# First half of the second feed-forward product's first sum in one lump early in the block, its other half later

## The chip, the cores and the metric

The kernel runs on one core of one Trainium2 chip. The metric is the device time of one execution in microseconds (us). The kernel before was run three times: 4296.52, 4300.87 and 4306.44 us, median 4300.87 us. One more execution, of 4298.3 us, was profiled, and all rows shown here come from it.

## The reference

A block of a transformer on x of shape (8, 1024, 512): eight sequences, called samples here, of 1024 tokens.

```
y   = x + attention(layernorm(x))        # differential attention, 16 heads, causal
out = y + (gelu(layernorm(y) @ W1q.T + b1) @ W2q.T + b2)
```

The attention projects queries (32 sub-heads of 16), keys and values, applies rotary embedding, takes two causal softmaxes a head, subtracts the second times a scalar from the first, multiplies by the values, normalises each head's output and projects with Wo. The feed-forward part has 2048 hidden features; W1q and W2q are the weights rounded to -1, 0 or 1, and gelu is the exact one.

## The kernel before, in words

A **block** is one tile of 128 query tokens against all keys up to it: 8 tiles a sample, t0 to t7, 64 blocks. The width of a row of scores grows from 128 in t0 to 1024 in t7. All five engines run the same list of blocks and meet by semaphores alone; within an engine the order is fixed by the program (a plain loop over **half heads**, numbered 0 to 31 in each block, two a head), so an instruction that waits holds up all that is behind it on its engine.

In each half head TensorE makes scores ahead (`SP_`, lines 852 and 853), VectorE takes the row's maximum (`NM`, 682 or, for t0 to t3 in pairs, 690), ScalarE the exponential (`E`, 554), VectorE subtracts the two softmaxes (`E`, 705), TensorE transposes the difference (`DP` and, from t4 on, `DX`, 864), ScalarE copies it (`DT`, 566), and at the end of each eight heads TensorE multiplies it by the values (`M`, 887). Score slots are few (four banks), so scores of a later softmax wait for the exponential of an earlier one.

Between these stand, at fixed half heads, the pieces of other work for neighbouring tiles: layernorm, transposes and projections of the next tile's queries, keys and values (`M` from `TOK`, `T`, and line 837 from `WQKV`), the previous tile's output (transposes of `T`, product with `WO`), and the feed-forward part, which is done for two tiles together (a **pair**):

- In odd blocks, the first product (line 909, into `F`): 8 pieces of two feature tiles (f) each, at the half heads `W1_AT`. The piece at half head `at` computes its first f there, its second at `at + 1`, and ScalarE empties both at `at + 2` (`HP`, line 613). One f is 8 matmuls. Each piece after the first waits until the one before has been emptied.
- Gelu on ScalarE (line 571), eight feature tiles at once: for the first half in half head 14 of the odd block (`GELU_ODD`), for the second half in half head 0 of the even block after it (`GELU_EVEN`). Each time it is between two loads of activation tables. GpSimd then splits each quarter of a half into a high and a low part (`HH`, `HP`, `HL`, lines 470, 472, 474), at half heads 15 to 18 of the odd block and 1 to 4 of the even one.
- In even blocks, the second product (line 924, into `F`): two **sums** j = 0 and 1 (one per tile of the pair), each over 16 f, with two matmuls an f (`HH` and `HL` against `W2Q`). The sums start at the half heads `W2_AT = (4, 18)` and are spread over 13 half heads, so one f or two in each. f 8 to 15 of the first sum wait for GpSimd's split of the second half (`h_ready`). VectorE takes the finished sum out of `F` (line 774) at half heads 17 and 31.

`F` is a single bank. Its users are in turn: the eight pieces of the first product, sum 0, sum 1. In TensorE's program a piece of either product stands behind the half head's transposes and projections and ahead of `scores_ahead` or `half_v`. At even half heads the order is: scores, transposes of differences, the second part of the value product, the layernorm and projection work, the feed-forward piece, the scores of the next head. The second product runs in 32 even blocks: t4 and t6 of the first sample, t0, t2, t4 and t6 of seven more, and two in the tail behind the last attention block.

Of the kernel before, what the change touches and what calls it, by code (L numbers as in the profile page):

```python
# [49 lines left out]
FT = FF // P  # L50
# [15 lines left out]
GELU_F = FT // 2  # L66
# [53 lines left out]
MEAN_SQ, RMS_ROWS, AN_TURN = 10, 14, 23  # L120
O_PROJ, O_SUM = (24, 25, 26, 27), 28
LN2_STATS, LN2_ROWS, LN2_TURN, LN2_REST = 28, 30, 31, 31
W1_AT = (1, 4, 7, 11, 15, 19, 23, 27)
GELU_ODD, GELU_EVEN = 14, 0
SPLIT_ODD, SPLIT_EVEN = (15, 16, 17, 18), (1, 2, 3, 4)
W2_AT, W2_N = (4, 18), 13
OUT_AT = (17, 31)


class QBlock:  # L130
# [25 lines left out]
    def first_product(self, hs):  # L156

        for k, at in enumerate(W1_AT if self.w1 else ()):
            if hs in (at, at + 1, at + 2):
# [2 lines left out]

    def second_product(self, hs):

        for j, at in enumerate(W2_AT if self.w2 else ()):
            if at <= hs < at + W2_N:
                return j, range(FT * (hs - at) // W2_N, FT * (hs - at + 1) // W2_N)
        return None


# [11 lines left out]
def diff_attention_ffn(nc, x, wqT, wkT, wvT, woT, lams, subw, w1T, b1, w2T, b2, rope, out):  # L182
    ctx = ExitStack()
    with ctx:
# [156 lines left out]
        def hold(eng, signal, value):  # L341


            if not isinstance(value, int) or value > 0:
                eng.wait_ge(signal, value)
                eng.sem_inc(held, 1)
# [480 lines left out]
        def _(pe):  # L827
# [85 lines left out]

            def second_product(q, j, fs):

                if fs[0] == 0:
                    hold(pe, h_ready, 8 * q + 4)
                    hold(pe, hp_ready, 8 * q + 8)
                    hold(pe, o_sum, 2 * q + j)
                for f in fs:  # L920
                    if f == GELU_F and j == 0:
                        hold(pe, h_ready, 8 * q + 8)
                    for hp in (HH, HL):
                        ins = pe.matmul(F[:, :], hp[:, f, P * j:P * (j + 1)], W2Q[:, f, :],  # L924
                                        start=(f == 0 and hp is HH), stop=(f == FT - 1 and hp is HL))
                if fs[-1] == FT - 1:
                    ins.then_inc(f2_ready, 1)

            def pe_work(T):
                b, t, nb, nf = T.b, T.t, T.nb, T.nf  # L930
                for hs in range(HS_TILE):
# [57 lines left out]
                    if T.second_product(hs):  # L989
                        second_product(T.pair, *T.second_product(hs))  # L990
# [67 lines left out]
```

## Time and profile before

| | before |
|---|---|
| runs | 4296.52, 4300.87, 4306.44 us |
| profiled execution, its span | 4298.3 us, 4296.5 us |
| mean granted TensorE clock | 0.926 |
| busy: TensorE, VectorE, ScalarE, GpSimd | 81%, 79%, 67%, 33% |
| wait of scores for an exponential (TensorE) | 385.4 us in 218 waits |

Busy shares are means over stages of a block that have different limits; a stage is read from the timeline of its own stretch. The timeline gives start and duration of an instruction in us, the engine, the line, the operation, what it writes and reads, the shapes, and in square brackets how long the engine was idle before it and what ended that. The windows view gives for a stretch its length, and for each engine the busy time and the number of instructions, then the granted clock (1.00 is 2.4 GHz, 0.50 is 1.2 GHz), the share of the DMA engines and GB/s.

### The profile page before, as it was taken

To read this page: it belongs to the slowest core of one execution; us is meant where nothing else is said; L and a number is where in the kernel's file an instruction comes from. 1 tells how busy PE (TensorE), PEld (TensorE's weight loads), DVE (VectorE), ACT (ScalarE), POOL (GpSimd) and SP (SyncE) were. 2 spreads that over 40 slices of the span, in tenths; PEclk is the share of its full clock that TensorE was granted. 3 is DMA by queue.
4 is the path that set the end of the run, shared out by engine and by line. 5 is a ranking of instruction groups with operands and counts; after the bars stand their busy time and mean duration, and the time that the engine had idled before them with its cause. 6 is when DMAs were issued, how large, how long until landed. Compare 5 with 4: busy or idle time off the path is not lost.

```text
span 4296.5 us, 81536 instructions
## 1 busy us (share of the span) xinstructions
PE 3484.7 (81%) x23454; PEld 2095.0 (49%) x23454; DVE 3382.8 (79%) x6194; ACT 2880.2 (67%) x6784; POOL 1437.2 (33%) x1564
## 2 busy tenths in 40 slices
PE   2688888888888887888788888888878878888886
PEld 1355544455445454545544544445544555444553
DVE  6788977888678886888767887778877889778881
ACT  1577766777567775677756777667766777567772
POOL 1243233332332324433343323432234432333323
PEclk6899999999999999999999999999999999999998
DMA  3100011000011001100011000101011000111000
GB/s 130 41 18 30 19 33 33 31 17 29 25 33 33 18 30 33 33 20 28 21 33 33 26 27 18 39 25 33 20 34 33 25 23 20 34 33 33 15 29 12
DMA packets 146817, 128.38 MB, mean 30 GB/s; under 512 B 66608, under 2 KB 117680, under 8 KB 145840
## 3 DMA queue, kind: packets, MB, share of 16 engines
q1 hardware_dynamic: 146352, 122.79, 8.8%
q8 instruction: 218, 3.57, 0.3%
q14 instruction: 247, 2.02, 0.2%
HBM read 67.61 MB, written 55.12 MB: 29 GB/s over the span
## 4 chain that ended last, share of the span: by engine, by line
PE 41%; DVE 20%; issue 20%; ACT 12%; POOL 5%; DMA 1%; SPq 1%; DVEq 1%; ACTq 1%; POOLq 0%
PE M L837 9%; DVE NM L682 6%; PE M L887 6%; PE SP_ L852 6%; PE F L924 6%; PE F L909 5%; PE DP L864 4%; DVE NM L690 3%; ACT E L554 3%; ACT DT L566 2%; ACT L571 2%; PE M L831 2%; DVE CC L702 1%; PE DX L864 1%; PE SP_ L853 1%
## 5 line engine op out<-in xcount | busy, mean ns | idle before, releaser
L554 ACT ACTIVATE E<-SP_,NM 128x256 f32<-128x256 f32 (+7 forms) x2048 | 1520.4, 743 | 1020.3 <-DVE NM L690 533.8
L852 PE MATMUL SP_<-KST,QST 96*128 96x512 f16 (+3 forms) x3072 | 838.2, 344 | 459.2 <-ACT E L554 385.4
L682 DVE TENSOR_REDUCE NM<-SP_ 128x1 f32<-128x896 f32 (+3 forms) x1024 | 1031.9, 1017 | 225.0 <-PE SP_ L853 218.5
L705 DVE SCALAR_TENSOR_TENSOR E<-E,CC 128x512 f32<-128x512 f32 (+7 forms) x1024 | 942.2, 920 | 36.2
L864 PE MATMUL DP<-ident,E 128*128 128x128 f32 x3328 | 585.1, 292 | 112.8 <-DVE E L705 97.2
L852 PEld LDWEIGHTS SP_<-KST,QST 96*128 96x128 f16 x3072 | 277.9, 101 | 793.8 <-ACT E L554 531.1
L690 DVE TENSOR_REDUCE NM<-SP_ 128x2 f32<-128x1024 f32 (+3 forms) x512 | 419.4, 819 | 244.8 <-PE SP_ L853 239.5
L566 ACT ACTIVATE DT<-DP 128x512 f32<-128x512 f32 (+3 forms) x1024 | 524.8, 513 | 127.8 <-PE DP L864 121.4
L837 PE MATMUL M<-WQKV,WT 128*128 128x512 f32 x1040 | 538.4, 611 | 10.3 <-DVE TOK L746 5.3
L909 PE MATMUL F<-X2H,W1Q 128*128 128x256 f16 x2048 | 501.4, 283 | 39.4 <-ACT HP L613 21.7
L864 PEld LDWEIGHTS DP<-ident,E 128*128 128x128 f32 x3328 | 389.8, 149 | 277.8 <-issue 125.8
L909 PE MATMUL F<-X2L,W1Q 128*128 128x256 f16 x2048 | 499.7, 282 | 0.0
L853 PE MATMUL SP_<-maskb,identb 128*128 128x128 bf16 x2048 | 450.9, 229 | 0.0
L450 POOL TENSOR_TENSOR RST<-VE,nhalf 128x1 f32<-128x1 f32 x129 | 70.9, 549 | 1113.8 <-DVE VE L644 1113.8
L554 ACT ACTIVATION_READ_ACCUMULATOR E<-SP_,NM 128x1 f32 x2048 | 413.0, 202 | 0.0
L924 PE MATMUL F<-W2Q,HH 128*128 128x512 fp8e4 x1024 | 389.8, 381 | 15.6 <-POOL HL L474 10.1
L924 PE MATMUL F<-W2Q,HL 128*128 128x512 fp8e4 x1024 | 388.9, 380 | 0.0
L887 PE MATMUL M<-DT,V 128*32 128x256 f32 x4608 | 318.5, 414 | 22.4 <-ACT DT L566 21.6
L474 POOL TENSOR_TENSOR HL<-HP,HH 128x512 f16<-128x512 f32 x256 | 318.3, 1243 | 21.4
L702 DVE TENSOR_SCALAR CC<-R,SUM,neglam 128x1 f32<-128x1 f32 x1024 | 279.3, 273 | 39.2 <-DVE R L700 2.1
L853 PEld LDWEIGHTS SP_<-maskb,identb 128*128 128x128 bf16 x2048 | 210.1, 103 | 182.2 <-issue 42.7
L837 PE MATMUL M<-WO,WT 128*128 128x512 f32 x512 | 271.8, 613 | 4.1 <-ACT WT L600 3.0
(94 smaller groups left out, 4726.9 us busy)
## 6 DMA issues: line engine op xcount, KB each, us to landing
scratch<-SPL SPq DMA_DIRECT2D x65, 576.0 KB, 2.8
QST<-scratch SPq DMA_DIRECT2D x390, 64.0 KB, 2.4
X<-in_x SPq DMA_DIRECT2D x66, 256.0 KB, 2.7
out<-SQ SPq DMA_DIRECT2D x64, 256.0 KB, 2.0
KST<-scratch SPq DMA_DIRECT2D x390, 32.0 KB, 1.9
DT<-in_w2T SPq DMA_DIRECT2D x1, 4096.0 KB, 25.7
KST<-in_w1T SPq DMA_DIRECT2D x2, 1024.0 KB, 12.0
WQKV<-in_wqT SPq DMA_DIRECT2D x1, 1024.0 KB, 7.1
```

The costliest lines, as they stand in the source:

```text
L554: act.activation(dst, score_out(i, 2 * n + k, w), ACT.Exp, bias=NM[:, (2 * u + k) % 8:(2 * u + k) % 8 + 1], scale=1.0, accum_out=SUM[:, i ...
L566: act.activation(DT[:, k0:k1, n % HALF, :], (DP, DX)[g][:, 0:P * (k1 - k0)].rearrange("p (k q) -> p k q", q=P), ACT.Copy).then_inc(dt_read ...
L682: nc.vector.tensor_reduce(NM[:, m:m + 1], score_out(i, 2 * n + k, P * (i + 1)), AX.X, ALU.max, negate=True).then_inc(max_ready, 1)
L690: nc.vector.tensor_reduce(NM[:, m:m + 2], SP_[:, k:k + 2, 0:P * (i + 1)], AX.X, ALU.max, negate=True).then_inc(max_ready, 2)
L705: nc.vector.scalar_tensor_tensor(out=E1[:, u % 4, 0:w], in0=E2[:, u % 2, 0:w], scalar=CC[:, u % 4:u % 4 + 1], in1=E1[:, u % 4, 0:w], op0=A ...
L837: ins = pe.matmul(M[:, :], WT[:, P * j:P * (j + 1)], w[:, j, c0:c0 + 512], start=(j == 0), stop=(j == KD - 1))
L852: pe.matmul(SP_[:, k[a // 512], 0:n], q, KST[0:ROWS, a // P:(a + n) // P, kk, :], start=True, stop=not last)
L853: ins = pe.matmul(SP_[:, k[(w - P) // 512], (w - P) % 512:(w - P) % 512 + P], identb[:, :], maskb[:, :], start=False, stop=True)
L864: ins = pe.transpose((DP, DX)[g][:, P * (k % 4):P * (k % 4 + 1)], E1[:, u % 4, P * k:P * (k + 1)], ident[:, :])
L887: ins = pe.matmul(M[DV * q:DV * (q + 1), 0:2 * P], V[:, k, v:v + DV], DT[:, k, 2 * q:2 * q + 2, :], start=(k == 0), stop=(k == i), skip_gr ...
L909: ins = pe.matmul(F[:, 2 * P * j:2 * P * (j + 1)], W1Q[:, c, P * f:P * (f + 1)], xp[:, c, :], start=(c == 0 and xp is X2H), stop=(c == KD ...
L924: ins = pe.matmul(F[:, :], hp[:, f, P * j:P * (j + 1)], W2Q[:, f, :], start=(f == 0 and hp is HH), stop=(f == FT - 1 and hp is HL))
```

## The change

Of the first sum (j = 0) of the second product, f 0 to 7 (16 matmuls) are issued together in half head 1 of the even block, and f 8 to 15 in half heads 10 to 16: one f each in 10 to 15 and two in 16. The second sum stays at 18 to 30. In odd blocks the pieces 4, 5 and 6 of the first product start at half heads 16, 20 and 24 in place of 15, 19 and 23.

```diff
-W1_AT = (1, 4, 7, 11, 15, 19, 23, 27)
+W1_AT = (1, 4, 7, 11, 16, 20, 24, 27)
-W2_AT, W2_N = (4, 18), 13
+W2_LUMP, W2_REST, W2_NEXT = 1, (10, 7), (18, 13)
...
     def second_product(self, hs):
-        for j, at in enumerate(W2_AT if self.w2 else ()):
-            if at <= hs < at + W2_N:
-                return j, range(FT * (hs - at) // W2_N, FT * (hs - at + 1) // W2_N)
+        if not self.w2:
+            return None
+        if hs == W2_LUMP:
+            return 0, range(0, GELU_F)
+        for j, f0, (at, n) in ((0, GELU_F, W2_REST), (1, 0, W2_NEXT)):
+            if at <= hs < at + n:
+                return j, range(f0 + (FT - f0) * (hs - at) // n, f0 + (FT - f0) * (hs - at + 1) // n)
         return None
...
             def second_product(q, j, fs):
+                if not fs:
+                    return
                 if fs[0] == 0:
```

## Rows read from the trace of the kernel before

**Rows 1.** The page: busy us of each engine.
```profile
PE 3484.7 (81%) x23454; PEld 2095.0 (49%) x23454; DVE 3382.8 (79%) x6194; ACT 2880.2 (67%) x6784; POOL 1437.2 (33%) x1564
```

**Rows 2.** Waits of TensorE: us in total, times, longest.
```profile
PE SP_ L852 <- ACT E L554: 385.4, 218, 5.5
PE F L924 <- POOL HL L474: 10.1, 2, 9.3
```

**Rows 3.** Windows, blocks t0, t2, t4, t6: TensorE done with half head 0, until released.
```profile
1607.90:1615.70 7.80, 1.13 (x6) 0.73 (x5) 3.86 (x11) 6.43 (x10) 2.38 (x4) 0.50 0.00 1
1712.50:1718.50 6.00, 1.16 (x5) 0.58 (x4) 2.59 (x6) 5.94 (x9) 2.03 (x4) 0.50 0.00 0
1829.00:1834.10 5.10, 0.02 (x1) 0.00 (x1) 1.83 (x5) 5.06 (x6) 2.31 (x4) 0.50 0.00 0
1968.20:1973.70 5.50, 0.02 (x1) 0.00 (x0) 2.61 (x5) 5.46 (x6) 2.51 (x4) 0.50 0.00 0
```

**Rows 4.** Windows, the same blocks: from that release until the clock rises.
```profile
1615.70:1619.90 4.20, 4.20 (x36) 2.57 (x40) 3.46 (x7) 2.17 (x8) 3.57 (x5) 0.50 0.02 4
1718.50:1722.30 3.80, 3.32 (x22) 1.61 (x23) 3.62 (x8) 2.08 (x8) 3.44 (x4) 0.50 0.00 0
1834.10:1838.40 4.30, 4.06 (x30) 2.43 (x34) 3.37 (x6) 2.09 (x5) 3.86 (x5) 0.51 0.03 6
1973.70:1978.30 4.60, 4.58 (x28) 2.70 (x32) 3.44 (x5) 3.08 (x7) 4.16 (x5) 0.50 0.02 4
```

**Rows 5.** Windows, the same blocks, half heads 5 to 12.
```profile
1623.00:1635.00 12.00, 11.51 (x63) 6.16 (x62) 7.65 (x22) 4.96 (x23) 6.58 (x6) 1.00 0.01 3
1723.10:1735.80 12.70, 11.91 (x63) 6.58 (x62) 10.13 (x21) 7.41 (x23) 8.43 (x9) 1.00 0.00 1
1841.20:1856.00 14.80, 13.76 (x78) 7.65 (x77) 13.72 (x26) 10.03 (x26) 7.14 (x6) 1.00 0.00 1
1982.00:1998.00 16.00, 15.80 (x90) 9.02 (x89) 15.50 (x25) 12.56 (x26) 5.97 (x4) 1.00 0.01 2
```

**Rows 6.** Timeline, second product at the full and at the half clock.
```profile
1628.01 0.38 PE L924 MATMUL F<-W2Q,HH 128*128 128x512 fp8e4 x1
1628.23 0.38 PE L924 MATMUL F<-W2Q,HL 128*128 128x512 fp8e4 x1
...
4279.34 0.63 PE L924 MATMUL F<-W2Q,HH 128*128 128x512 fp8e4 x1
4279.76 0.63 PE L924 MATMUL F<-W2Q,HL 128*128 128x512 fp8e4 x1
```

**Rows 7.** Timeline, block t0: behind the release, then to the query projection.
```profile
1615.69 1.11 PE L864 MATMUL DX<-ident,E 128*128 128x128 f32 x4 [3.67 <-ACT DT L566]
1617.16 3.26 PE L887 MATMUL M<-DT,V 128*32 128x256 f32 x32
1620.61 1.93 PE L887 MATMUL M<-DT,V 128*32 128x256 f32 x32
...
1623.69 0.60 PE L831 MATMUL M<-ident,TOK 128*128 128x128 f32 x4
...
1626.65 1.10 PE L837 MATMUL M<-WQKV,WT 128*128 128x512 f32 x2 [0.39 <-DVE TOK L746]
```

**Rows 8.** Timeline, block t2: GpSimd's last split; second product in half head 10.
```profile
1727.07 1.16 POOL L474 TENSOR_TENSOR HL<-HP,HH 128x512 f16<-128x512 f32 x1
...
1732.33 0.38 PE L924 MATMUL F<-W2Q,HH 128*128 128x512 fp8e4 x1
```

**Rows 9.** Timeline, VectorE: one instruction away from and beside GpSimd's split.
```profile
1139.34 0.54 DVE L648 TENSOR_SCALAR TOK<-X,MV,RST 128x512 f32<-128x512 f32 x1
...
1837.00 1.38 DVE L648 TENSOR_SCALAR TOK<-X,MV,RST 128x512 f32<-128x512 f32 x1
```

**Rows 10.** Timeline, block t5: TensorE's waits in half heads 16 and 18.
```profile
1930.97 0.82 PE L852 MATMUL SP_<-KST,QST 96*128 96x512 f16 x2 [2.81 <-ACT E L554]
...
1937.70 0.50 PE L852 MATMUL SP_<-KST,QST 96*128 96x512 f16 x2 [1.34 <-ACT E L554]
```

## The prediction

> **What bounds the kernel now.** I read the page first, then TensorE's waits, then windows and timelines of one sample's even blocks (t0, t2, t4, t6 of the fourth; the blocks repeat in all seven samples of the loop). TensorE is busy 3484.7 of 4296.5 us and VectorE 3382.8 [rows 1], so neither is the bound by its sum alone; where each is has to be read by stage. The longest wait of TensorE is that of scores for an exponential, 385.4 us in all, with a longest of 5.5 [rows 2]. The windows show where it lies: in each even block TensorE is through with half head 0 and then has next to nothing to do for 5.1 to 7.8 us, while ScalarE is busy all along (5.06 of 5.10 in t4) with a table load, the gelu of half a hidden tile, and another table load [rows 3]. In this stretch the granted clock is 0.50, and after the release it stays there for another 3.8 to 4.6 us although TensorE is then almost always busy (4.20 of 4.20 us in t0) [rows 4]. Behind that, in half heads 5 to 12, TensorE is the busiest engine: 11.51 of 12.00 us in t0, 11.91 of 12.70, 13.76 of 14.80, and 15.80 of 16.00 in t6 [rows 5]. But VectorE closes up on it: idle for 4.35 us of that stretch in t0, 2.57 in t2, 1.08 in t4, 0.50 in t6. So work taken from TensorE there pays in full in t0 at best, and in t6 hardly.
>
> **The lump.** It adds nothing and removes nothing: 16 matmuls a block go from half heads 4 to 9 (seven f) and 12 (one f; half head 10 keeps one) to half head 1. Two matmuls of this kind start 0.22 us apart at the full clock and 0.42 at the half [rows 6], so the lump takes 16 x 0.215 = 3.4 us or 16 x 0.425 = 6.8 us. What it needs is there: f 0 to 7 were split in the odd block before, and `F` was emptied at half head 29 of it. The clock is at 0.50 when the lump starts. In the four rows it rose 4.20, 3.80, 4.30 and 4.60 us after TensorE had resumed [rows 4]; I take 4.2 us, that is 10 matmuls at 0.425, and 6 at 0.215: 5.5 us. Bounds are 3.4 and 6.8.
>
> The room for it, less what TensorE did in it: 7.80 - 1.13 = 6.7 us in t0, 6.00 - 1.16 = 4.8 in t2, 5.1 in t4, 5.5 in t6 [rows 3]. So with 5.5 us the lump overruns by 0.7 in t2, 0.4 in t4 and not in t0 and t6; behind it wait the scores and transposes of half head 2, and for these ScalarE's copy and VectorE's maximum. This is more than given back by the clock, which is now at 1.00 when that work comes. In t0, the value product of 32 matmuls took 3.26 us at the half clock and 1.93 at the full one a moment later, and the four transposes ahead of it 1.11 against 0.60 for four of the same shape at the full clock (line 831) [rows 7]; 1.33 + 0.51 = 1.8 us earlier. All of it would be on TensorE's path in t0, since the next scores stand behind the value product. In t2 it is half of that product (16 matmuls, 0.7 us saved), in t4 and t6 VectorE has its own queue there. I take head gains of 1.8 us in t0, 0.3 net in t2, 0.6 in t4 and 0.5 in t6 (bounds: 0 and 1.8 each, and minus 2.0 if the clock does not come up, below).
>
> The same VectorE instruction took 0.54 us away from GpSimd's split and 1.38 us beside it in t4's head [rows 9]. The Trainium skill, "SBUF — State Buffer", section "Who interferes with whom", says that VectorE and GpSimd share one pair of ports and that whichever starts first keeps the other out for the whole instruction. By that rule of the Trainium skill alone VectorE would be held to GpSimd's pace in the heads of t4 and t6, the splits being where they were, and the head gains of these two would be 0 in place of 0.6 and 0.5; the sum below would be 4298.3 - 43 = 4255 us for the profiled execution.
>
> **The relief in half heads 4 to 12.** One f costs TensorE 2 x 0.215 = 0.43 us there; eight are 3.4 us a block. Not all of it is on the path. From the layernorm transposes of half head 6 (1623.69) to the query projection (1626.65) are 2.96 us in t0 [rows 7]: transposes 0.60, copy on ScalarE 0.60, transposes of the attention output, VectorE's multiplication, each waiting for the one before; two f stand in it and fill waits. Without them TensorE waits 0.86 us more, so these two give nothing. For the f of half head 12 I count nothing either, since the key projection behind it needs VectorE's rotation of the queries (bounds 0 and 0.43). That leaves five f, 2.15 us. In t0 VectorE has 4.35 us of slack and takes it; I deduct 0.6 for ScalarE, whose copy at half head 6 stands behind an exponential: 1.8 + 2.15 - 0.6 = 3.3 us. In t2 the slack is 2.57 us, of which part is round trips that stay; I take 1.0 and with the head 1.3. In t4 VectorE's slack is 1.08: 0.6 here, 1.2 with the head. In t6 0.50: 0.3, and 0.8 with the head. Each is bounded by 0 and by 2.15 + 0.43 + 0.86 = 3.4.
>
> **The other half.** f 8 now stands in half head 10, one earlier, and waits for GpSimd's last split. In t2, where this is closest, that split ends at 1728.2 and the second product of half head 10 is at 1732.3 [rows 8], so with f 8 there and 1.5 us earlier it has 2.6 us to spare. It costs nothing, unless half head 10 comes over 4 us earlier. In the tail, f 8 waits for GpSimd as it is (two waits, 10.1 us [rows 2]) and all of the lump's gain ends in that wait: 0.
>
> **Pieces 4 to 6 of the first product.** In each odd block one f (8 matmuls) leaves the gelu stretch of half head 15 and goes to half head 17, another goes from 19 to 21. TensorE's wait in half head 16 grows by 0.87 us (2.81 us in t5), at no cost, since the release is the exponential. The f now in half head 17 delays the scores of 18 by 0.87 us, but the wait of 1.34 us in the same half head absorbs that [rows 10], and ScalarE empties `F` one half head later, so that the exponential for which TensorE waits comes up to 0.8 us sooner. Against it: a longer gap, after which the clock may fall where it did not. I take +0.5 us a sample for the four odd blocks together, bounds -3 and +3.
>
> **Sum.** 3.3 + 1.3 + 1.2 + 0.8 + 0.5 = 7.1 us a sample, times 7 = 49.7; the first sample has t4, t6 and their neighbours only: 2.3. Together 52 us. 4298.3 - 52 = 4246 for the profiled execution, 2.6 us below the median of the runs, so 4249 us against a median of 4300.9.
>
> **The rivals.**
> 1. TensorE is the bound all through, and VectorE's slack is no limit. Then 3.4 us of relief in each of 30 blocks, 102 us, less the two f of the latency chain (26 us), and the heads (3.2 us a sample, 24 us): 100 us, 4201 us. For it: TensorE's busy share in rows 5. Against it: VectorE's, in t4 and t6.
> 2. VectorE and the round trips are the bound outside t0, and heads are eaten by the overrun. Then t0 alone gives 2 to 3.3 us: 7 x 2.5 = 18 us, 4283 us. For it: VectorE's 13.72 of 14.80 and 15.50 of 16.00 us. Against it: the slack that it still has in t2.
> 3. Slower: the clock stays at the half through the lump. It takes 6.8 us in a room of 6.7, 4.8, 5.1 and 5.5: overruns of 0.1, 2.0, 1.7 and 1.3 us, which hold scores and transposes of half head 2 and with them every engine. 7 x 2.1 + 8 x 3.0 = 39 us, and the relief is lost because VectorE starts late and cannot catch up: 4340 us. It decides from the point where the overrun (5.1 us a sample) exceeds the relief that VectorE can take. Against it: a lump is denser than what raised the clock in rows 4.
> 4. No change that can be told: the gains of t0 go into later waits of the same block, and odd blocks lose as much. 4299 us.
>
> **How the numbers follow.** Forecast 0.63, rival 1 0.14, rival 2 0.11, rival 3 0.07, rival 4 0.05. What a measurement of this kernel can tell from no change is 0.2%, 8.6 us. Faster: 0.63 + 0.14 + 0.10 = 0.87; within 0.2%: 0.06; slower: 0.07. The forecast's own range is 4225 to 4275 by the bounds on t2, t4 and t6; with the better part of rivals 1 and 2, 4207 to 4285.
>
> **What would show it.** In the changed profile: 16 matmuls of line 924 in a row inside the gelu stretch of each even block, the last six or so 0.22 us apart; the granted clock at 1.00 from half head 2 on, and the 32-matmul value product of t0 at 1.9 us; a longer wait for the attention-side multiplication ahead of t0's query projection, over 1 us in place of 0.39; VectorE nearly gapless in t6; the mean granted clock above 0.926. Block t0 shorter by 3.3 us, t6 by 0.8, odd blocks as before. The prediction is wrong if the first scores of half head 2 come later by more than 1 us in t2 or t4, if f 8 waits for `HL` inside the loop, or if the odd blocks get longer by over 0.5 us each.

## The result, and the profile after

The changed kernel takes 4275.64 us (median of 4 runs, 4273.97 to 4279.57), against 4303.65 for the kernel before beside it (4 runs, 4296.52 to 4306.97): a ratio of 0.9938, interval 0.9925 to 0.995. That is 28 us faster, 4276 where 4249 was forecast. The side was right, the size only about half of the forecast's 52 us, and the time lies at the edge of the forecast's own range, 0.6 us above its upper end of 4275 (it is inside the wider 4207 to 4285, which takes in the better part of rivals 1 and 2). The profiled execution took 4276.51 us, with a span of 4274.7 us and a mean granted clock of 0.946.

The page after, busy us of each engine, to be read against [rows 1]:

```profile
PE 3496.3 (82%) x23454; PEld 2087.9 (49%) x23454; DVE 3397.1 (79%) x6194; ACT 2883.5 (67%) x6784; POOL 1440.0 (34%) x1564
```

The counts of instructions are the same, and each engine's busy time is within 15 us of what it was. Nothing was taken off an engine; work was moved into waits. TensorE's waits after, to be read against [rows 2] (line numbers are 4 higher in the changed kernel):

```profile
PE SP_ L856 <- ACT E L558: 341.4, 271, 3.8
...
PE M L891 <- ACT DT L570: 47.5, 59, 2.0
...
PE F L930 <- POOL HL L478: 14.6, 2, 9.3
PE M L841 <- ACT WT L604: 12.1, 16, 1.0
...
PE F L930 <- issue: 8.8, 6, 2.8
```

The scores' wait fell by 44 us, to a longest of 3.8. Three waits grew: those of the value product for its copy (21.6 us before), of the products of line 841 for theirs (3.0 before) and of `F` for `HL` (10.1 before, again two, both in the tail). The windows of the gelu stretch, same blocks as [rows 3]:

```profile
1602.50:1611.30 8.80, 5.84 (x23) 2.41 (x21) 3.87 (x11) 6.44 (x10) 2.39 (x4) 0.64 0.00 1
1704.50:1710.70 6.20, 5.68 (x23) 2.31 (x21) 2.71 (x8) 6.14 (x9) 2.12 (x4) 0.74 0.00 0
1820.60:1825.80 5.20, 5.17 (x19) 1.78 (x16) 1.93 (x5) 5.16 (x6) 2.31 (x4) 0.69 0.00 0
1956.80:1962.40 5.60, 5.28 (x19) 1.89 (x18) 2.68 (x5) 5.56 (x6) 2.55 (x4) 0.70 0.01 3
```

Here as in all windows the first pair of times is the stretch, then come its length and the busy time of TensorE, of its weight loads, of VectorE, ScalarE and GpSimd, and the granted clock. TensorE is now busy for 5.17 to 5.84 us in each, where it was for 0.02 to 1.16, and the clock comes up inside the stretch. Behind it, from the end of half head 4 to the key projection of half head 13 (nearly the stretch of [rows 5]):

```profile
1616.70:1626.20 9.50, 7.75 (x42) 4.16 (x41) 7.31 (x20) 5.04 (x24) 7.30 (x7) 1.00 0.01 3
1713.70:1726.00 12.30, 9.36 (x51) 5.40 (x51) 11.51 (x23) 8.42 (x26) 10.21 (x10) 1.00 0.01 2
1832.10:1846.30 14.20, 12.55 (x68) 7.29 (x67) 13.16 (x25) 10.10 (x26) 7.21 (x7) 0.88 0.00 1
1970.00:1986.10 16.10, 13.39 (x75) 7.46 (x75) 15.51 (x25) 12.57 (x26) 6.69 (x5) 1.00 0.01 2
```

Drawn over the same instructions in the trace of before:

```profile
1623.30:1634.20 10.90, 10.41 (x57) 5.54 (x55) 6.92 (x20) 4.66 (x22) 5.50 (x4) 1.00 0.01 3
1723.30:1736.20 12.90, 12.11 (x65) 6.74 (x63) 10.49 (x22) 7.54 (x23) 8.70 (x8) 1.00 0.00 1
1841.20:1856.20 15.00, 13.96 (x80) 7.75 (x79) 13.89 (x27) 10.13 (x27) 7.34 (x6) 1.00 0.00 1
1982.80:1998.60 15.80, 15.60 (x89) 8.94 (x87) 15.30 (x24) 11.82 (x25) 5.77 (x4) 1.00 0.01 2
```

TensorE was idle for 0.2 to 1.0 us in these and now is for 1.65 to 2.9. In t6 VectorE is busy for 15.51 of 16.10 us: the bound has passed to it, and the block gains nothing there. Its 0.62 us are all gained by half head 6.

To see where time went I measured each block from its first exponential to the next block's first, and took the mean over the samples 2 to 7. Change against before, us:

```
                        t0     t1     t2     t3     t4     t5     t6     t7    sum
before, length       52.77  50.30  56.27  58.61  67.01  72.17  76.67  85.08  518.9
forecast              -3.3    (odd)  -1.3           -1.2           -0.8      odd -0.5
changed kernel       -3.32  +0.58  -0.75  +1.50  -1.37  -0.49  -0.62  +0.12  -4.35
second product only  -3.20  +0.04  -1.67  +0.01  -1.53  +0.04  -0.05  +0.08  -6.28
```

Even blocks: -6.1 of the 6.6 us forecast. Odd blocks: +1.7 where -0.5 was forecast. Over the whole profiled execution (forecasts in brackets): even blocks of the loop -39.8 (-46.2), odd ones +12.1 (-3.5), the first sample +0.8 (-2.3), the stretch ahead of it +1.1 (0), and from the last block on +4.1 (0); together -21.8 us (-52). So of the 30 us that are missing half are the odd blocks'. The profiled executions compared here differ by less than the medians (21.8 against 28 us): the one of before is 5 us below the median beside the changed kernel.

### The profile page after: what moved, and what is told of

The parts are those of the page before. It is cut to its first block, busy times and chain, and to the rows that moved or that the text cites. A ratio compares the mean times of both kernels' runs of the same rounds, so it can differ in the third digit from the quotient of the medians.

```text
span 4274.7 us, 81536 instructions
## 1 busy us (share of the span) xinstructions
PE 3496.3 (82%) x23454; PEld 2087.9 (49%) x23454; DVE 3397.1 (79%) x6194; ACT 2883.5 (67%) x6784; POOL 1440.0 (34%) x1564
## 3 DMA queue, kind: packets, MB, share of 16 engines
q8 instruction: 218, 3.57, 0.4%
## 4 chain that ended last, share of the span: by engine, by line
PE 37%; DVE 23%; issue 22%; ACT 10%; POOL 4%; DMA 2%; SPq 1%; DVEq 1%; ACTq 1%; POOLq 0%
PE M L841 8%; DVE NM L686 8%; PE SP_ L856 6%; PE F L913 6%; PE F L930 5%; PE M L891 5%; PE DP L868 4%; DVE NM L694 3%; ACT E L558 2%; DVE CC L706 2%; ACT DT L570 2%; PE M L835 2%; ACT L575 2%; DVE E L709 2%; PE DX L868 1%
## 5 line engine op out<-in xcount | busy, mean ns | idle before, releaser
L856 PE MATMUL SP_<-KST,QST 96*128 96x512 f16 (+3 forms) x3072 | 824.1, 339 | 415.3 <-ACT E L558 341.4
L709 DVE SCALAR_TENSOR_TENSOR E<-E,CC 128x512 f32<-128x512 f32 (+7 forms) x1024 | 959.7, 937 | 36.2
L856 PEld LDWEIGHTS SP_<-KST,QST 96*128 96x128 f16 x3072 | 269.0, 100 | 768.6 <-ACT E L558 535.6
L868 PE MATMUL DP<-ident,E 128*128 128x128 f32 x3328 | 567.7, 285 | 93.8 <-DVE E L709 83.9
L841 PE MATMUL M<-WQKV,WT 128*128 128x512 f32 x1040 | 547.2, 620 | 16.5 <-DVE TOK L750 9.8
L868 PEld LDWEIGHTS DP<-ident,E 128*128 128x128 f32 x3328 | 381.2, 145 | 255.2 <-issue 128.6
L930 PE MATMUL F<-W2Q,HH 128*128 128x512 fp8e4 x1024 | 419.3, 409 | 28.8 <-POOL HL L478 14.6
L930 PE MATMUL F<-W2Q,HL 128*128 128x512 fp8e4 x1024 | 417.0, 407 | 0.0
L891 PE MATMUL M<-DT,V 128*32 128x256 f32 x4608 | 289.5, 384 | 48.8 <-ACT DT L570 47.5
L478 POOL TENSOR_TENSOR HL<-HP,HH 128x512 f16<-128x512 f32 x256 | 309.2, 1208 | 21.4
L841 PE MATMUL M<-WO,WT 128*128 128x512 f32 x512 | 273.0, 615 | 13.1 <-ACT WT L604 12.1
```

What stands on the lines that cost most here:

```text
L709: nc.vector.scalar_tensor_tensor(out=E1[:, u % 4, 0:w], in0=E2[:, u % 2, 0:w], scalar=CC[:, u % 4:u % 4 + 1], in1=E1[:, u % 4, 0:w], op0=A ...
L841: ins = pe.matmul(M[:, :], WT[:, P * j:P * (j + 1)], w[:, j, c0:c0 + 512], start=(j == 0), stop=(j == KD - 1))
L856: pe.matmul(SP_[:, k[a // 512], 0:n], q, KST[0:ROWS, a // P:(a + n) // P, kk, :], start=True, stop=not last)
L868: ins = pe.transpose((DP, DX)[g][:, P * (k % 4):P * (k % 4 + 1)], E1[:, u % 4, P * k:P * (k + 1)], ident[:, :])
L891: ins = pe.matmul(M[DV * q:DV * (q + 1), 0:2 * P], V[:, k, v:v + DV], DT[:, k, 2 * q:2 * q + 2, :], start=(k == 0), stop=(k == i), skip_gr ...
```

## The experiments

**1. Second product only.** The changed kernel with the first product's pieces put back.

```diff
-W1_AT = (1, 4, 7, 11, 16, 20, 24, 27)
+W1_AT = (1, 4, 7, 11, 15, 19, 23, 27)
```

> The changed kernel with the pieces 4 to 6 of the first product back at half heads 15, 19 and 23; the lump and the later half of the first sum stay. Theory A (the odd blocks lose through the moved pieces: +1.7 us a sample in the profile where I had counted -0.5): the odd blocks t1, t3, t5, t7 are as long as before, 50.3, 58.6, 72.2, 76.7+8.4 us, the even ones keep what they gained (t0 -3.3, t2 -0.75, t4 -1.4, t6 -0.6), and the time is 4275.6 - 8 x 1.7 = 4262 us. Rival B (the odd blocks are longer because the even blocks before them reach them in another state, with GpSimd or the clock): t3 stays 1.5 us longer than before and the time 4276 us.

4256.89 us, ratio 0.9878 (0.9864 to 0.9892), 52 us faster than before. Its row stands in the table: the odd blocks are as before within 0.1 us, the even ones carry all. So moving the pieces costs some 25 us (0.9938 against 0.9878) in place of bringing 3.5. In the profiled executions it is 19.7 us (4274.7 against 4255.0): 10.7 in the odd blocks of the loop and 6.3 in the even ones, above all in t2 (-0.75 against -1.67 us), whose program is the same in both kernels.

**2. First product only.** The kernel before with pieces 4, 5 and 6 at half heads 16, 20 and 24.

> The kernel before with the pieces 4 to 6 of the first product moved to 16, 20 and 24, the second product as it was. Theory A: t3 is longer by 1.5 us in every sample, t1 by 0.6, t5 and t7 between -0.5 and +0.1, sum +1.7 x 8 = +14: 4317 us against 4303.7, even blocks as before. Rival B: no change, 4304 us. My forecast's step on record (these moves give 0.5 us a sample): 4300 us.

4335.6, ratio 1.006 (1.0047 to 1.0073): 27 us slower. By blocks t0 to t7: +0.20, +0.11, +0.61, +1.59, +0.45, +0.29, +0.71, +1.02. The cost does not need the lump. It was twice what I expected, in part because the even blocks, whose code is that of before, got longer as well (+14.2 us in the loop, the odd ones +20.9); the time at the half clock in the whole span went from 639 to 694 us.

**3. Piece 6 put back.** The changed kernel with (..., 16, 20, 23, 27).

> The changed kernel with piece 6 alone back at half head 23; pieces 4 and 5 stay at 16 and 20. Theory A1: the loss is made by piece 6, whose second f now ends only in half head 25, so that ScalarE's emptying of it in half head 26 stands late and in front of the exponential of 27 (+1.4 us there in every odd block), while pieces 4 and 5 had won up to 1.8 us in t5 and 1 us in t7 until then. Then the odd blocks come out shorter than before: t3 by 0 to 0.9, t5 by 1.5, t7 by 0.7 us, and the time is 4275.6 - 8 x 4 x 1.2 = 4237 us at best, 4255 if half of it is lost again. Rival A2: pieces 4 and 5 make the loss too: 4270 us or more.

4269.77, 0.9912 (0.99 to 0.9925). Halfway: pieces 4 and 5 together cost some 14 us over experiment 1, and piece 6 another 11. Against experiment 1 the blocks t1, t3, t5, t7 differ by +0.82, +0.86, -0.86 and -0.28.

**4. The lump as an extra.** The kernel before, with f 0 to 7 computed once more in half head 1 (the second computation, in half heads 4 to 10, overwrites it).

```diff
+                    if T.w2 and hs == 1:
+                        second_product(T.pair, 0, range(0, GELU_F), True)
```

> The kernel before with f 0 to 7 of the first sum computed once more, in half head 1 (16 matmuls more in each even block), and the whole sum as before in 4 to 16. It measures the head alone: the clock that the lump brings up, less its overrun. My forecast's terms: t0 -1.8, t2 -0.3, t4 -0.6, t6 -0.5 us, 3.2 a sample, 4303.7 - 24 = 4280 us, and half heads 5 to 12 as before. Rival (the lump only overruns, what it gains is relief): no gain or up to +1 us in t2 and t4, 4304 to 4320 us.

4295.2, 0.9957 (0.994 to 0.9973). The heads gained only 0.4, 0.6, 0.8 and 0.6 us in t0, t2, t4 and t6, and t3, t5 and t7 lost 0.8, 0.5 and 0.6, though nothing was changed in them. In t2, t4 and t6 that is the head gain of the forecast (0.3, 0.6 and 0.5). In t0 it is far from the 1.8 expected; why is seen from its timeline in sample 4 (start us, length, instruction, idle before):

```profile
1604.17 0.63 PE L924 MATMUL F<-W2Q,HH 128*128 128x512 fp8e4 x1
...
1608.51 0.38 PE L924 MATMUL F<-W2Q,HL 128*128 128x512 fp8e4 x1
...
1611.69 0.66 PE L864 MATMUL DX<-ident,E 128*128 128x128 f32 x4 [2.37 <-ACT DT L566]
1612.70 3.21 PE L887 MATMUL M<-DT,V 128*32 128x256 f32 x32
```

and that of the changed kernel:

```profile
1602.36 0.31 PE L857 MATMUL SP_<-maskb,identb 128*128 128x128 bf16 x1
1605.51 0.59 PE L930 MATMUL F<-W2Q,HH 128*128 128x512 fp8e4 x1 [2.85 <-issue]
...
1608.84 0.38 PE L930 MATMUL F<-W2Q,HH 128*128 128x512 fp8e4 x1
...
1610.35 0.38 PE L930 MATMUL F<-W2Q,HL 128*128 128x512 fp8e4 x1
...
1612.29 1.93 PE L891 MATMUL M<-DT,V 128*32 128x256 f32 x32
```

In the changed kernel the lump starts 2.85 us after TensorE has run dry, although nothing that it waits for shows, and ends when the exponentials come: the value product runs at the full clock, 1.93 us. In experiment 4 it starts at once, is through early, TensorE idles for 2.37 us, and the same product takes 3.21. The other samples say that the end of the lump counts and not its late start. In experiment 4 the lump ends 2.37 to 3.38 us early in six of the seven, the product takes 3.21 to 3.57 us and t0 gains at most 0.24; in sample 2 it ends at the release (a wait of 0.19 us), the product takes 1.93 and t0 gains 1.61. Experiment 1 has the reverse in sample 2: the lump ends 2.27 us early, the product takes 3.52, and t0 gains 1.84 us where it gains 3.3 to 3.6 in the others.

**5. The relief alone.** Experiment 1 without the lump, f 0 to 7 of the first sum left out altogether (so its output is another).

> The kernel of e1_second_only (first product as before) without the lump: f 0 to 7 of the first sum are left out, the sum is f 8 to 15 only. So it has the relief of half heads 4 to 12 and no lump, and nothing brings the clock up in the gelu stretch. Theory (head and relief add up): e1 less the head measured by the extra lump (t0 -0.4, t2 -0.6, t4 -0.8, t6 -0.6), so t0 -2.9, t2 -1.1, t4 -0.7, t6 0: 4.7 us a sample, 4308.6 - 35 = 4274 us, slower than e1 although it does less. Rival (all is relief, the lump costs what the clock gives): 4256 us or less, even blocks t0 -3.3, t2 -1.7, t4 -1.5. My forecast's terms would give t0 -1.5, t2 -1.0, t4 -0.6, t6 -0.3.

4288.63, 0.9947 (0.9933 to 0.996). t0, t2 and t4 gained 1.40, 1.14 and 0.77 us; t6 changed by less than 0.1 in four of the loop's seven samples (+0.5 in the mean). The expectation, that this and experiment 4 add up to experiment 1 in t0 (so 2.9 here), fell: it took experiment 4's t0 for the head's gain, which the early lump had spoiled. What does add up is this: experiment 1 less experiment 5 is 1.8 in t0, 0.5 in t2, 0.8 in t4 and 0.6 in t6, which are the prediction's four head gains (1.8, 0.3, 0.6, 0.5), and the relief is its 1.5, 1.0, 0.6 and 0.3.

**6. A lump of six.** Experiment 1, with f 6 and 7 in half heads 6 and 7.

> e1_second_only with a lump of f 0 to 5 (12 matmuls) and f 6 and 7 in half heads 6 and 7, where the copy, the transposes, the multiplication and the query projection wait for one another. Theory (what stands in that chain of waits is free): t0, t2 and t4 as long as in e1, within 0.2 us, and the time 4257 us; the lump ends 0.9 us earlier. Rival (TensorE is the bound there as well): 0.86 us more in each even block where VectorE has slack, t0 and t2 at least, 4257 + 14 to 26 = 4271 to 4283 us.

4258.57, 0.9872 (0.9857 to 0.9887): as experiment 1. In t0 (-3.3 to -3.6 in five of seven samples, in six there) and in t2 the two f in the chain of half heads 6 to 8 are free, as the prediction said; t4 lost most of its relief (-0.39 in place of -1.53).

**7. Piece 6 only.** Experiment 1 with (..., 15, 19, 24, 27).

> e1_second_only with piece 6 alone moved, from half head 23 to 24. Theory (its first f in half head 23 covers the wait from the transposes of the normalised output over ScalarE's copy to the product with WO; moved away, the wait stands bare): t3 +0.7 us, t1, t5 and t7 between 0 and 0.7, so 8 x 1.4 = 11 us more than e1: 4268 us. The wait of WO for that copy, 0.2 us a block before, becomes 0.6. Rival (only pieces 4 and 5 cost, piece 6 merely shifts): 4257 us.

4281.27, 0.9929 (0.9916 to 0.9943): 22 us slower than experiment 1, twice the expected. The blocks t3, t5 and t7 are 1.25, 0.76 and 0.82 us longer than there, t1 is not; in the profiled executions a third of the cost (7.5 of 25.5 us) is in even blocks, 0.95 us of it in each t2. The same instructions of t3, half heads 23 to 26, first in experiment 1, then here:

```profile
1790.78 0.66 PE L835 MATMUL M<-ident,TOK 128*128 128x128 f32 x4 [0.26 <-DVE T L681]
1791.28 0.27 PE L913 MATMUL F<-X2H,W1Q 128*128 128x256 f16 x1
...
1792.15 0.60 PE L868 MATMUL DP<-ident,E 128*128 128x128 f32 x4
1792.98 1.12 PE L841 MATMUL M<-WO,WT 128*128 128x512 f32 x2 [0.23 <-ACT WT L604]
...
1797.58 0.38 PE L856 MATMUL SP_<-KST,QST 96*128 96x512 f16 x1
```

```profile
1799.08 0.66 PE L835 MATMUL M<-ident,TOK 128*128 128x128 f32 x4 [0.26 <-DVE T L681]
1800.32 0.65 PE L868 MATMUL DP<-ident,E 128*128 128x128 f32 x4 [0.58 <-DVE E L709]
1801.28 1.12 PE L841 MATMUL M<-WO,WT 128*128 128x512 f32 x2 [0.31 <-ACT WT L604]
...
1804.59 0.27 PE L913 MATMUL F<-X2H,W1Q 128*128 128x256 f16 x1
...
1806.76 0.38 PE L856 MATMUL SP_<-KST,QST 96*128 96x512 f16 x1
```

From the first transposes to the scores of half head 26 are 6.80 us there and 7.68 here, 0.88 more: one f of 8 matmuls, 0.87 us. In experiment 1 piece 6's first f stands between these transposes and the next ones, in time in which TensorE would otherwise wait (0.58 for VectorE's difference). It was free there: to the product with `WO` are 2.20 us with it and 2.20 without. Moved on by one half head, it leaves that wait open, and its second f now stands in half head 25, ahead of the scores of 26, where TensorE waits for nothing. From half head 27 on t3 is 0.9 us behind in all seven samples; the rest of its 1.25 (0 to 0.8 us a sample) comes between its last exponential and the next block's first, and its cause is open.

**8. Piece 4 earlier.** Experiment 1 with piece 4 computed in half heads 14 and 15 and emptied in 17 as before, and the tail's order as before.

```diff
-W1_AT = (1, 4, 7, 11, 15, 19, 23, 27)
+W1_AT = (1, 4, 7, 11, 14, 19, 23, 27)
+W1_LATE = 4
...
+            if hs == at + 2 + (k == W1_LATE):
+                return k, 2
+        if not self.attend and hs < W2_NEXT[0]:
+            return (0, range(FT * (hs - 4) // 13, FT * (hs - 3) // 13)) if 4 <= hs < 17 else None
```

> e1_second_only with two edits. Piece 4 of the first product at half heads 14 and 15 in place of 15 and 16, emptied by ScalarE in 17 as before, so that in t5 and t7, where TensorE waits for ScalarE's gelu at the start of half head 16, both its f stand under that wait; and in the tail the first sum is spread over half heads 4 to 16 as in the kernel before. Theory (work moved under the gelu's wait is free, 0.87 us an f): t5 and t7 shorter by 0.9 us each, t1 and t3 as they are, where both f already stood ahead of the wait; 8 x 1.7 = 14 us; the tail gives back 4 us: 4257 - 18 = 4239 us. Rival (t5 and t7 are held by VectorE behind the gelu and gain nothing): the tail's 4 us alone, 4253 us.

4254.58, 0.986 (0.9845 to 0.9875), within the interval of experiment 1. Of the 18 us expected it brought none that can be told: t5 gained 0.94 us, t7 nothing, and t2 and t4 gained 0.7 and 0.3 less than there, so that the profiled executions are even (4256.93 and 4256.75). The tail has the order of before in it and is as long as in experiment 1 (101.4 us behind the last exponential, against 101.9; 98.4 before), so that order is not what made it longer.

**9. Piece 4 only** (..., 16, 19, 23, 27), and **10. piece 5 only** (..., 15, 20, 23, 27).

> e1_second_only with piece 4 alone moved, from half head 15 to 16. Theory (work taken out from under the gelu's wait costs its whole length, 0.87 us an f, in a block where TensorE is the bound behind it): t3 +0.87, t1 +0 to 0.5, t5 and t7 between -0.4 and +0.4, since there a wait of 1.3 us in half head 18 takes it up; 8 x 1.3 = 10 us over e1, ratio to the kernel before 0.990. Rival (the pieces 4 and 5 cost only as a pair, through ScalarE's later emptying): no difference from e1, 0.988.

> e1_second_only with piece 5 alone moved, from half head 19 to 20. Its first f stays ahead of the same waits but one, the value product of half head 19, its second goes behind the transposes of the keys in 21. Theory (nothing was covered by it, TensorE is busy on both sides): within 2 us of e1 in t3, t5 and t7, ratio 0.987 to 0.989. Rival (piece 5 makes what e3_piece6_back lost against e1, 13 us): 0.991.

Piece 5 alone: 4261.76, 0.9885 (0.987 to 0.99), as experiment 1 in the whole. But its t3 is 0.8 us longer than there in every one of the seven samples (t5 and t7 are 0.2 and 0.4 shorter in the mean): I had expected that this piece covered nothing, and it did cover a wait, as is seen below. Piece 4 alone: 4304.45, 0.9986 (0.9977 to 0.9995), nearly 50 us slower than experiment 1, so the pieces' costs are far from additive. With piece 4 later and piece 5 where it was, `F` has to be emptied between them just when piece 5 starts. In TensorE's waits:

```profile
PE F L913 <- ACT HP L617: 49.3, 69, 3.8
```

against 21.8 us in 53 in experiment 1. In t3's half head 19 of experiment 9, sample 4:

```profile
1803.67 0.27 PE L913 MATMUL F<-X2H,W1Q 128*128 128x256 f16 x1 [1.84 <-ACT HP L617]
...
1804.63 3.43 PE L891 MATMUL M<-DT,V 128*32 128x256 f32 x32
```

and in windows over the wait and over the product behind it:

```profile
1801.50:1804.60 3.10, 1.26 (x11) 0.71 (x8) 3.03 (x5) 2.66 (x7) 2.74 (x4) 1.00 0.00 0
1804.60:1808.10 3.50, 3.50 (x34) 1.53 (x34) 2.65 (x4) 0.78 (x2) 3.17 (x5) 0.54 0.00 0
```

The wait is 1.84 us where it was 0.51 in experiment 1, the clock falls right behind it, and the value product takes 3.43 us where it took 1.93. This block is 3.0 us longer than in experiment 1. That is not the rule, though. Five of the seven samples have the wait of 1.84, and in three of them the clock stays up, as here in sample 2:

```profile
765.71 0.27 PE L913 MATMUL F<-X2H,W1Q 128*128 128x256 f16 x1 [1.84 <-ACT HP L617]
...
766.68 1.93 PE L891 MATMUL M<-DT,V 128*32 128x256 f32 x32
```

In these three t3 is 1.4 us longer: the uncovered wait costs 1.4 us, and the fall of the clock, in two samples, another 1.6. (The other two samples wait 0.44 and 0.95 us there and are 1.4 and 2.0 us longer.) In the mean t3 is 2.0 us longer than in experiment 1, and t7 as much; there the wait for `HP` is 0.64 us in every sample and the product takes 1.93, so t7's loss has another cause, which is open. In the changed kernel piece 5 went along by one half head, so this wait does not arise; another does:

```profile
1794.43 1.93 PE L891 MATMUL M<-DT,V 128*32 128x256 f32 x32 [1.02 <-ACT DT L570]
```

This is the value product of t3's half head 19: piece 5's first f stood ahead of it and covered that wait. Five of the seven samples have it, with 1.02 us. Experiment 10, where the first f is moved away as well, has it in all seven, with 1.57 us, and the product takes 1.93 all the same:

```profile
1787.43 1.93 PE L891 MATMUL M<-DT,V 128*32 128x256 f32 x32 [1.57 <-ACT DT L570]
```

In experiment 1 the same product starts 0.03 us after the f ahead of it.

**11. A filler in piece 6's old place.** Experiment 7, with the first f of piece 6 computed once more in half head 23.

> e7_piece6_only with the first f of piece 6 computed once more in half head 23, where it stood in the kernel before, 8 matmuls more in each of 32 odd blocks; its real place stays 24. Theory (an f in half head 23 stands in the wait from the transposes over ScalarE's copy to the product with WO, so it is free there): the same time as e7_piece6_only within 4 us, ratio 0.993 to 0.994, and the wait of WO for the copy as short as in the kernel before. Rival (TensorE is the bound in half head 23 too): 32 x 0.87 = 28 us more, ratio 0.9995.

4296.18, 0.9962 (0.995 to 0.9974), 14 us slower than experiment 7. Against experiment 1, t3, t5 and t7 are +1.06, +0.20 and +1.01, against +1.25, +0.76 and +0.82 in experiment 7: in t3, t5 and t7 the filler costs nothing. The 14 us are in t0 (+1.16) and t1 (+1.36). The edit does not touch t0. It does touch t1, whose half head 23 has the filler too, but in four of the seven samples t1 is 1.2 to 1.6 us behind experiment 7 at exponential 21 already, ahead of the filler; the other three lose theirs behind its last exponential, and why is open. In t0:

```profile
1613.78 0.88 PE L868 MATMUL DX<-ident,E 128*128 128x128 f32 x4 [2.64 <-ACT DT L570]
...
1615.01 3.12 PE L891 MATMUL M<-DT,V 128*32 128x256 f32 x32
```

As in experiment 4, the lump has no gap ahead of it, leaves a wait of 2.64 us behind it, and the value product takes 3.12 us. Six of the seven samples are so (2.68 to 3.30 us).

**12. The best of these together.** Experiment 8, with f 6 and 7 in half heads 6 and 7 in the blocks t0 and t2.

> e8_piece4_early (0.986) with f 6 and 7 of the first sum in half heads 6 and 7 in t0 and t2, where they are free, and all eight f in the lump in t4 and t6. Theory: in t2 the holes that the lump leaves in half heads 6 and 7 let the clock fall in some samples (t2 between -1.9 and +0.9 us against the kernel before); with an f in each they don't, t2 gives 1.8 us in every sample, 8 x 0.8 = 6 us less than e8: ratio 0.9845. Rival: the clock falls or not by other things and t2 scatters as before, ratio 0.986.

4246.35, 0.9856 (0.9841 to 0.9871): the lowest median of this study, 0.8% faster than the changed kernel, though its interval overlaps those of experiments 1, 6, 8, 10 and 13, so that the gain over experiment 8 (0.0015 expected, 0.0004 measured) cannot be told from none. t2 is now -1.75 to -1.93 us in all seven samples of the loop; in the changed kernel it runs from -1.9 to +1.0, in experiment 1 it is -0.7 once and -1.8 to -1.9 otherwise. On the other side t3 is 1.2 us longer than before in five of the seven, whose cause is open.

**13. Only the emptying of piece 6 later.** Experiment 1, with ScalarE's emptying of piece 6 in half head 26 in place of 25. If piece 6's cost were ScalarE's order (the emptying now stands ahead of another exponential), it would show here; if it is TensorE's, not.

> e1_second_only with TensorE's program untouched (piece 6 at half heads 23 and 24) and only ScalarE's emptying of piece 6 moved, from half head 25 to 26. Theory S (the cost of piece 6 is ScalarE's: in half head 25 the emptying, 0.85 us, lies in ScalarE's wait for the maximum ahead of exponential 26; in 26 it stands between the exponentials 26 and 27, where ScalarE has no wait): each odd block is longer by 0.7 to 0.9 us as in e7_piece6_only, most of it between exponential 26 and 27, and the ratio to the kernel before is 0.993 as there. Rival T (TensorE's f in half head 25, or the uncovered wait in 23, made it): as e1_second_only, ratio 0.988.

4255.02, 0.9884 (0.9867 to 0.99), every odd block within 0.3 us of experiment 1. ScalarE's rows in t3, half heads 26 and 27:

```profile
1800.30 0.84 ACT L620 ACTIVATE HP<-F,b1c 128x256 f32<-128x256 f32 x2
1801.01 0.70 ACT L561 ACTIVATE E<-SP_,NM 128x512 f32<-128x512 f32 x1
```

The exponential of half head 27 starts 1.87 us after that of 26 (1.15 in experiment 1), held by the emptying, and the block is no longer: ScalarE has the room. The cost of piece 6 is TensorE's.

## Why the prediction was right and where it was wrong

**The lump: right.** In t0 it took 5.2 us (1605.51 to 1610.73) where 5.5 were forecast, and the clock came up inside it. The value product took 1.93 us. The overrun forecast for t2 and t4 (0.7 and 0.4 us) does not show: none of their first exponentials comes later than before. That in t0 the lump also ended at the release was partly luck, which the forecast had not counted on (experiments 4 and 11). The head gains forecast were 1.8, 0.3, 0.6 and 0.5; experiment 1 less experiment 5 gives 1.8, 0.5, 0.8 and 0.6. That is also the answer to the Trainium skill's rule ("SBUF — State Buffer", section "Who interferes with whom"), by which the heads of t4 and t6 were to gain nothing: they gained, though VectorE's instruction beside GpSimd's split is as slow as in [rows 9] (1.38 us in t4 of the changed kernel). I had read that rule too widely. The same section of the Trainium skill exempts `tensor_reduce` on this chip. The row maxima are such instructions, 1448 of VectorE's 3397 us. The trace agrees: in the changed kernel the maximum over 128x768 takes 0.96 us away from GpSimd's instructions and 0.95 beside them (medians).

Rival 3 (the lump stays cold, 4340 us) fell with the clock of the windows, 0.64 to 0.74 in the mean over the stretch.

**The relief: right in t0, t2 and t4.** 1.5, 1.0, 0.6 and 0.3 forecast; 1.4, 1.1 and 0.8 measured (experiment 5), and in t6 nothing: 0 in four samples, a loss of 0.3 to 1.3 in three. The two f of half heads 6 to 8 counted as free in t0 are so (experiment 6). The wait ahead of the query projection of t0 is

```profile
1620.01 1.10 PE L841 MATMUL M<-WQKV,WT 128*128 128x512 f32 x2 [0.82 <-DVE TOK L750]
```

0.82 us against "over 1" forecast and 0.39 in [rows 7]. VectorE bounds t6, as said. The second product's move by itself brought 52 us, against 46.2 + 2.3 = 48.5 in my sum for it. So close a fit is partly luck: in the profiled executions it brought 41.5, of which the even blocks of the loop 46.1 as forecast, the first sample 0.5 in place of 2.3, and the tail took 3.9; within the even blocks t2 and t4 gave 0.4 and 0.3 us more and t6 0.75 less than forecast.

**The clock "at 1.00 from half head 2 on": only partly right.** It was so in most, but the relief leaves holes, and in some samples the clock falls behind one. In t4 of the fourth sample:

```profile
1832.00:1834.10 2.10, 1.07 (x12) 0.82 (x10) 2.10 (x4) 1.38 (x6) 1.82 (x3) 0.99 0.00 0
1834.10:1837.50 3.40, 3.25 (x17) 2.09 (x15) 2.54 (x5) 2.70 (x7) 1.46 (x2) 0.50 0.01 2
```

Two waits of 1.0 us stand ahead of that fall. In t2 the mean of -0.75 is one of values between -1.9 and +1.0. Experiment 12, which fills the hole of half heads 6 and 7, was steady in that block, but experiment 1, with the same hole as the changed kernel, nearly so. That the clock falls behind short waits in some samples is seen; that the holes are the cause, and that they make the spread of t2, is not shown. I had asked about the clock in the odd blocks' longer gap and not in the holes which the relief itself makes.

**Pieces 4 to 6: wrong, and this is the step that failed.** The prediction gave "+0.5 us a sample" as a gain for the four odd blocks together. They lost 1.7, and the whole edit costs 25 us of the 52. Its own sign of being wrong, an odd block longer by over 0.5 us, is met by t3 (+1.50) and just so by t1 (+0.58). Three things were wrong in it.
- Piece 6 was counted nowhere: the text speaks of f going from 15 to 17 and from 19 to 21, not of the one from 23 to 25. It is the most plainly shown cost, 0.88 us in t3 in all seven samples (experiment 7; 13 excludes ScalarE).
- The absorption of the f in half head 17 was read from t5 alone [rows 10] and is seen only there: pieces 4 and 5 together gave -0.86 us in t5 and +0.82 and +0.86 in t1 and t3 (experiment 3), which have no such wait behind half head 17. t7 has one, of 1.25 us, but its -0.28 is within its scatter from sample to sample.
- What each f covered in its old place was not asked. The one in 19 covered a wait of the value product in t3, 1.57 us in experiment 10 and 1.02 in the changed kernel; that in 23 covered 0.58 and was free in full. The one in 15 covered nothing, as I had said (the release is the exponential).

Not all of the 25 us is in the odd blocks: in t2, which no edit of the pieces touches, the changed kernel gains 0.9 us less than experiment 1. Its cause is open.

**The tail and the ends: wrong by 8 us.** Forecast 0 for the tail; from the last block's start on it took 4.1 us more, the stretch ahead of the first block 1.1, and the first sample lost 0.8 in place of gaining 2.3, whose cause is open. The tail is not the lump's doing alone: 101.7 us behind the last exponential without it (experiment 5), 101.4 with the order of before (experiment 8), 97.9 with it (experiment 7), 98.4 before and 102.0 after. The waits for `HL` change with it (10.1 before, 14.6 after, 17.7 and 13.0 in experiments 5 and 7) and so does the time at the half clock (31.3, 34.2, 41.3, 24.6 us); which of them comes first was not settled. Nor was it settled why piece 4 alone costs 2.0 us in t7, nor how the single pieces' 3, 22 and 47 us make 25 together, beyond that piece 5's move takes away the wait which piece 4's makes.

## What to carry to other kernels

- A filler on an engine that works in order is free only where it covers a wait. Of each one that is moved, ask in every block it occurs in what it covered in its old place, and what stands behind it in its new one; shifts of one half head (two f of 0.87 us each) moved this kernel by between 3 and 47 us.
- A lump fits a stretch in which another engine alone is busy, and is worth most if it ends at the release: it then also brings TensorE's clock up for what follows (1.93 in place of 3.2 us for the same product). Where it ended 2.3 us or more ahead of the release, in experiments 1, 4 and 11, that was lost.
- Try the parts of a change apart. Here one part gave 52 us and the other took half of it back.

## What the runs showed of the hardware that was not expected

- TensorE's lump in t0, the first block of the loop's body, starts late with no semaphore that it waits for: by 0, 0.39, 2.85, 1.20, 1.36, 1.62 and 1.37 us in the seven samples of the changed kernel, by up to 2.89 in experiment 6, and never in experiments 4 and 11, in the same place of the order. The DMA records point at the loading of instructions. In all 60 late starts (six samples each of the changed kernel and nine experiments) the lump's first matmul comes 2.9 to 3.7 us after the start, and 1.9 to 2.2 after the end, of a 16 KB transfer on the queue that the page calls "q8 instruction"; in sample 4 of the changed kernel it is 3.10 and 2.13 us. In the loop's first sample, where no start is late, none stands in that place, and in experiments 4 and 11 the lump starts as little as 1.1 us after one has begun. No experiment varied it, so the cause is likely and not shown.
- The length of a wait did not decide by itself whether the clock fell. Behind the wait of 1.84 us in t3 of experiment 9 the value product took 1.93 us in three samples and 3.43 and 3.59 in two. Behind the lump in t0, a wait of 1.99 us was followed by a product of 1.93 (experiment 12, sample 5) and one of 1.98 by a product of 3.28 (experiment 6, sample 7). Waits of 1.57 in experiment 10 and of 1.02 in the changed kernel were followed by 1.93 each time.
- An edit in the odd blocks changes the time of even ones (experiments 2, 7 and 11), without a changed instruction there. In experiment 11 this goes through the clock in t0: 3.12 in place of 1.93 us for the value product. So a difference of 0.3% between two orders may lie in blocks that the edit does not touch, and only the block by block comparison tells that from a cost of the edit.
